# A gated delta layer: the decay table by a broadcast transfer and biased exponentials instead of matmuls

## The chip, the cores and the metric

The program runs on one core of one Trainium2 chip. The metric is the device time of one execution in microseconds (us). The kernel before has three runs; the median is what the kernel after is held against.

## What is computed

Two layers over `x` of 2 batches x 512 tokens x 256 features. Nearly all the time goes to the first: a gated delta rule with 16 key heads of 128, two value heads for each, and chunks of 64 tokens. For each head (T is a chunk's tokens):

```python
g = jnp.cumsum(g, axis=-1)                       # per chunk
diff = g[..., :, None] - g[..., None, :]
decay = jnp.where(tri, jnp.exp(jnp.where(tri, diff, 0.0)), 0.0)
M = jnp.where(tri_s, jnp.einsum('bhnci,bhndi->bhncd', k_b, k) * decay, 0.0)
Tinv = solve_triangular(eye + M, eye, lower=True)
u, w = Tinv @ v_b, Tinv @ (k_b * jnp.exp(g)[..., None])
attn_loc = jnp.where(tri, jnp.einsum('bhnci,bhndi->bhncd', q, k) * decay, 0.0)
# scan over chunks: v_new = u - w @ S; o = qg @ S + attn_loc @ v_new; S = S * exp(g_last) + kdecay^T @ v_new
og = o * silu(z); og = og * rsqrt(mean(og * og) + EPS) * norm_w;  y = og @ W_out
```

`q`, `k`, `v` go through a convolution of 4 taps and a silu first. Beside it stands a feed-forward layer with ternary weights (`f0`); then comes a second layer (attention, experts, a second ternary feed-forward), which the change leaves as it is.

## The kernel before

**Tiling.** The kernel works in blocks of 128 tokens, so a head has 2 batches x 4 blocks (`NT` = 8), and with its two value heads 16 tables of 128 x 128 (`HC` = 16). Everything is fp32. `gdn` holds the first layer. Each engine has its own streams of work, one generator per kind and head (`pe_decays`, `pe_key`, `pe_query`, `pe_value`, `pe_inverse`, `pe_z`, `pe_recur`, `pe_finish` on TensorE, and their fellows on the others).

**What sets the order.** Each piece of a stream yields a due time from a table written by hand (`AT` for heads 1 to 14, `FIRST` for head 0, `FINAL` for head 15, `START` for what runs once); head k adds `TURN * k`. `in_order` (L75) then puts the pieces of one engine in the order of their due times. So the tables set each engine's program order, and no more: on the chip an engine goes through its own list and waits on semaphores. The work of several heads is interleaved: while head k+1 makes its keys, queries and values, head k is inverted and runs its recurrence.

**One head.** `g_d` in device memory holds the cumulated gates of all heads as three bf16 parts.

- Decay table `E` (L545 to L557, L792 to L796): SyncE loads the head's rows of `g_d` into `GL` and `GR` (L478, L479). TensorE makes the differences in banks 2 and 3, four tables at a time: one matmul of 512 columns with the mask `later` (-1e30 above the diagonal), then four of 128 columns with the parts of g. ScalarE takes the exponential of 512 columns at once (L796). `E` is one buffer, so this waits for the last use of head k-1 (`AT`, L1000).
- Keys: projection (L542), first tap on ScalarE (L783), three taps on VectorE (L943), silu (L788), transposes into banks 2 and 3 (L571), squares and copies `kt` by ScalarE (L808, L815), scores k.k (L580). VectorE forms the norms (L948 to L973), GpSimd multiplies `E` by -beta/norm (`nE`, L1125), VectorE multiplies the scores by it: `CM` (L981).
- Queries likewise: scores q.k (L580) times `E` are `A` (L1000). Values: projections (L542), taps, transposes (L591), `vn` (L847).
- Inverse of I+M: `CM` goes to device memory and back as blocks of 16 (L507, L516), VectorE solves them (L1025 to L1031), they come back by DMA as `Td` (L525), and TensorE doubles the block size in `pe_inverse` (P16, TU16, P32, TU32, P64, U64: L597, L640, L647, L650, L653) with copies by ScalarE and VectorE between, all in banks 2 and 3. The scratch of it is `Td`, `Ud`, `P2`, `Tf`, `P4`, and the result is `UB`.
- Recurrence (L703 to L739): 8 steps (4 blocks x 2 batches); gate `z` (L690, L886); output: `og` is multiplied, normalised, transposed (L753), copied as `oT` (L935), projected (L761) and added to `yacc` (L1116).

GpSimd also does the ternary rounding of the f0 weights during head 0 and 1 (L1223 to L1231), and the f0 matmuls (L1367) fill TensorE during the recurrence of head 15.

## Time and profile before

| what | us |
|---|---|
| median of 3 runs | 1554.03 |
| lowest, highest run | 1548.35, 1557.99 |
| span of the profiled execution | 1551.7 |
| TensorE busy in it | 1401.1 (90%) |
| VectorE busy | 1046.9 (67%) |
| ScalarE busy | 865.6 (56%) |
| GpSimd busy | 534.3 (34%) |

The profiled execution's own time is its span from first to last instruction, 1551.7 us, with nothing else listed around it; it lies 2.3 us under the median. Busy shares are averages over stages that differ: until 120 us the heads start, until some 1100 us one head follows another in a steady pattern, until 1250 us the last head runs beside f0, and after it comes the second layer. A matmul's record includes its way through the array, so the time that a row of equal matmuls costs is read from start to start, not from the mean of one. One fp32 matmul of the program is two in the trace.

### The profile page before, as it was taken

Reading aid. Unit: us, or ns where it says so; the run is one execution under the profiler, and the core shown is the slowest. Engines: PE = TensorE matmul, PEld = TensorE weight load, DVE = VectorE, ACT = ScalarE, POOL = GpSimd, SP = SyncE. Lnnn points to the kernel's source line nnn. Section 1 sums busy time; section 2 is a strip of 40 time slices with the busy share of each in tenths; the row PEclk is TensorE's granted clock in tenths of the full one; section 3 lists DMA queues with packets and bytes.
Section 4 is the critical chain, followed back from the end, with each engine's and each line's share of the span. In section 5 each row is a group of like instructions: output and inputs, shape, how many; then the busy total and the mean of one; then the engine's idle time right before and its main releaser. Section 6 shows DMA issues by size and latency. Waiting matters only on the chain. (4 is left out here: it accounts for less than half of the span.)

```text
span 1551.7 us, 35674 instructions
## 1 busy us (share of the span) xinstructions
PE 1401.1 (90%) x13996; PEld 1045.2 (67%) x13996; DVE 1046.9 (67%) x2132; ACT 865.6 (56%) x1740; POOL 534.3 (34%) x562
## 2 busy tenths in 40 slices
PE   4569999999999999999999999999899977998998
PEld 3335767777776777777677777777578754555855
DVE  4887686877868687786858778686735544773344
ACT  5555656666666665666666666666355316676210
POOL 1872332342323233233323323333335446541100
PEclk9678999999999999999999999999989988999999
DMA  5112020201202021020102102110311130002100
GB/s 168 37 49 59 9 39 16 67 22 20 41 14 38 16 67 29 13 46 21 27 16 66 29 13 45 23 25 21 91 36 44 41 89 1 1 1 52 31 14 14
DMA packets 142486, 56.39 MB, mean 36 GB/s; under 512 B 109776, under 2 KB 134992, under 8 KB 142064
## 3 DMA queue, kind: packets, MB, share of 16 engines
q1 hardware_dynamic: 133424, 48.20, 13.4%
q10 hardware_dynamic: 8896, 5.91, 1.2%
q8 instruction: 113, 1.85, 0.5%
q14 instruction: 53, 0.43, 0.1%
HBM read 37.11 MB, written 16.97 MB: 35 GB/s over the span
## 5 line engine op out<-in xcount | busy, mean ns | idle before, releaser
L1153 POOL TENSOR_TENSOR og<-og,sz 128x256 f32<-128x256 f32 x128 | 93.3, 729 | 518.8 <-DVE og L1096 300.9
L690 PE MATMUL banks<-wz,xT 128*128 128x256 f32 x512 | 129.2, 397 | 13.8 <-DVE yacc L1116 13.8
L943 DVE SCALAR_TENSOR_TENSOR Yv<-banks,cwall,Yv 128x511 f32<-128x511 f32 (+2 forms) x192 | 130.3, 740 | 7.5 <-ACT Yv L783 7.4
L542 PE MATMUL banks<-wv,xT 128*128 128x512 f32 x256 | 121.5, 619 | 11.1 <-DVE Yv L943 9.6
L761 PE MATMUL banks<-wo,oT 128*128 128x256 f32 x512 | 123.8, 385 | 0.0
L542 PE MATMUL banks<-wqk,xT 128*128 128x512 f32 x256 | 121.7, 610 | 0.2 <-DVE Yk L943 0.2
L690 PEld LDWEIGHTS banks<-wz,xT 128*128 128x128 f32 x512 | 96.3, 196 | 36.6 <-issue 23.9
L930 ACT ACTIVATE junk<-og 128x512 f32<-128x512 f32 x64 | 40.6, 634 | 121.1 <-POOL og L1153 121.1
L1160 POOL TENSOR_TENSOR rn<-ss,c_half 128x4 f32<-128x4 f32 x64 | 64.5, 1007 | 122.0 <-DVE ss L1110 122.0
L761 PEld LDWEIGHTS banks<-wo,oT 128*128 128x128 f32 x512 | 93.6, 192 | 11.9 <-issue 0.7
L734 PE MATMUL banks<-V,A 128*128 128x128 f32 x512 | 85.8, 290 | 9.1 <-ACT V L910 9.1
L542 PEld LDWEIGHTS banks<-wv,xT 128*128 128x128 f32 x256 | 48.1, 198 | 61.6 <-issue 61.5
L1882 DVE TENSOR_REDUCE mx<-banks 128x1 f32<-128x128 f32 (+3 forms) x128 | 57.4, 487 | 43.5 <-PE banks L1805 43.1
L1082 DVE TENSOR_TENSOR St<-Sd,banks 128x256 f32<-128x256 f32 x64 | 26.9, 420 | 84.6 <-PE banks L739 84.6
L1125 POOL TENSOR_TENSOR E<-E,nsk 128x1024 f32<-128x1024 f32 x32 | 60.0, 1897 | 68.8 <-DVE nsk L970 51.3
L1107 DVE TENSOR_REDUCE ss<-junk 128x4 f32<-128x512 f32 x64 | 43.8, 684 | 56.9 <-ACT junk L930 56.9
L734 PEld LDWEIGHTS banks<-V,A 128*128 128x128 f32 x512 | 69.3, 191 | 18.5 <-ACT V L910 14.0
L542 PEld LDWEIGHTS banks<-wqk,xT 128*128 128x128 f32 x256 | 48.5, 196 | 43.4 <-issue 41.9
L935 ACT ACTIVATE oT<-banks,nw 128x512 f32<-128x512 f32 x64 | 44.4, 694 | 58.9 <-PE banks L753 58.9
L910 ACT COPY V<-banks 128x256 f32<-128x256 f32 x128 | 47.8, 374 | 48.2 <-PE banks L721 48.1
L943 DVE SCALAR_TENSOR_TENSOR Yk<-banks,cwall,Yk 128x511 f32<-128x511 f32 (+2 forms) x96 | 64.5, 740 | 6.1 <-ACT Yk L783 6.1
L721 PEld LDWEIGHTS banks<-R,UB 128*128 128x128 f32 x384 | 55.5, 193 | 19.3 <-issue 12.0
(380 smaller groups left out, 3663.2 us busy)
## 6 DMA issues: line engine op xcount, KB each, us to landing
cm_d<-CM SPq DMA_DIRECT2D x32, 256.0 KB, 4.0
wqk<-in_L_attn_W_qkvz SPq DMA_DIRECT2D x8, 512.0 KB, 4.6
wv<-in_L_attn_W_qkvz SPq DMA_DIRECT2D x8, 512.0 KB, 4.2
wz<-in_L_attn_W_qkvz SPq DMA_DIRECT2D x16, 256.0 KB, 2.9
wo<-in_L_attn_W_out SPq DMA_DIRECT2D x16, 256.0 KB, 3.1
blk<-cm_d SPq DMA_DIRECT2D x128, 16.0 KB, 1.8
t_d<-tb SPq DMA_DIRECT2D x16, 128.0 KB, 1.7
Td<-t_d SPq DMA_DIRECT2D x128, 16.0 KB, 1.9
```

Of the source, the lines that this page charges most:

```text
L542: ins = pe.matmul(bank[b][:, :], xT[:, d, b * S + of_batch, :], w[:, d, :], start=(d == 0), stop=(d == KD - 1))
L690: ins = pe.matmul(bank[7][:, b * 256:(b + 1) * 256], xT[:, d, b * S + q, :], wz[:, d, :], start=(d == 0), stop=(d == KD - 1))
L721: ins = pe.matmul(pV[:, h * DH:(h + 1) * DH], UB[k % 2][:, h * NT + n, :], R[b][:, h, :] if q else vn[k % 2][:, n, h, :], start=True, stop ...
L734: ins = pe.matmul(pK[:, h * DH:(h + 1) * DH], A[k % 2][:, h, n, :], V0[b][:, h, :], start=True, stop=True)
L761: ins = pe.matmul(bank[7][:, b * D:(b + 1) * D], oT[:, b, h, :], wo[k % 2][:, h, :], start=(h == 0), stop=(h == VR - 1))
L910: act.copy(V0[b][:, :, :], bank[6][:, 0:256].rearrange("p (h d) -> p h d", h=VR)).then_inc(s["V0"].sem, 1)
L935: act.activation(oT[:, :, :, :], bank[7][:, :].rearrange("p (b h t) -> p b h t", b=B, h=VR), ACT.Copy, scale=m["nw"][:, 0:1]).then_inc(s[" ...
L943: v.scalar_tensor_tensor(y, bank[b][:, 0:T - j], conv_w(k, t)[:, 3 - j:4 - j], y, ALU.mult, ALU.add).then_inc(s["tap"].sem, 1)
L1125: pool.tensor_tensor(E[:, h, :, :], E[:, h, :, :], nsk[:, h, :].unsqueeze(2).to_broadcast([P, NT, P]), ALU.mult).then_inc(s["nE"].sem, 1)
L1153: pool.tensor_tensor(og[:, n, :, :], og[:, n, :, :], sz[q % 2][:, b, :].rearrange("p (h d) -> p h d", h=VR), ALU.mult).then_inc(s["osz"].s ...
L1160: pool.tensor_tensor(rn[:, q, :, :], ss[:, q, :, :], c["neghalf"][:, 0:B * VR].rearrange("p (b h) -> p b h", b=B), ALU.pow).then_inc(s["rn ...
L1882: v.tensor_reduce(x[:, t, g:g + 1], top[i % 2][:, 0:(t + 1) * P], AX, ALU.max).then_inc(s["mx"].sem, 1)
```

## The change

1. The table `E` is made without TensorE. `g_d` keeps g as one fp32 row per head; SyncE loads it with one transfer that repeats the row to all 128 partitions, straight into `E` (1 MB a head). GpSimd adds the mask `later` (2 additions of 128 x 1024 a head, `pool_decays`), and ScalarE takes 16 exponentials of 128 x 128 in place, each with its own column of -g (`ngc`) as bias. `GL`, `GR`, their fills, the split into three bf16 parts and the 5 x 4 matmuls a head are gone.
2. The room goes to a second `CM`, and `Yq` gets a third buffer; `Tf` and `P4` become one tile `TP`.
3. With two `CM`, head k+1's k.k scores and `CM` come ahead of the inverse of head k: `P16` of head k now waits for `CM(1, k+1)`, and the k transposes of head k+1 no more for the end of head k's inverse but for `AT(1, k)`.
4. All due times of the first layer are new.

```diff
-    m["g_d"] = nc.dram_tensor("g_d", [3, HK, HC * P], BF16, kind="Internal").ap()
+    m["g_d"] = dram("g_d", [HK, HC * P])
+    m["ngc"] = sb("ngc", [P, W])
...
-        parts = Chain(v, s["pgp"])
+        v.tensor_scalar(m["ngc"][:, :], gc[:, :], -1.0, None, ALU.mult)
         yield START["gp"]
         v.wait_ge(*s["pgT"]())
-        v.tensor_copy(gT[:, :], bank[3][:, 0:W])
-        for i in range(3):
-            parts.step(v.tensor_copy(gp[:, i, :], bank[3][:, 0:W] if i == 0 else gT[:, :]))
-            if i < 2:
-                parts.step(v.tensor_tensor(gT[:, :], gT[:, :], gp[:, i, :], ALU.subtract))
+        v.tensor_copy(gT[:, :], bank[3][:, 0:W]).then_inc(s["pgp"].sem, 1)
...
-    "g": 115, "wqk": 137.01, "wv": 72.92, "cm": 160.76, "base": 209.71, "wz": 212.85, "E0": -33.56, "E1": -232.02, "E2": -29.83, "E3": -159.44, "exp0": -30.71, "exp1": -68.85,
+    "g": 14.39, "wqk": -22.77, "wv": 13.04, "cm": 30.79, "base": 76.04, "wz": 145.51, "E0": 10.19, "E1": 10.19, "exp0": 14.97, "exp1": 18.53, "exp2": 18.53, "exp3": 19.85,
...
         if k:
-            sp.wait_ge(*s["Ep"](3, k - 1))
+            sp.wait_ge(*s["AT"](1, k - 1))
         else:
-            sp.wait_ge(*s["zero"](1))
             sp.wait_ge(*s["pg_d"]())
-        sp.dma_start(GL[0:3, :, :], m["g_d"][:, k, :].rearrange("r (m t) -> r m t", t=P)).then_inc(s["gl"].sem, 16)
-        sp.dma_start(GR[3:6, :, :], m["g_d"][:, k, :].rearrange("r (m t) -> r m t", t=P)).then_inc(s["gl"].sem, 16)
+        sp.dma_start(Ef.rearrange("p m t -> p (m t)"), m["g_d"][k, :].partition_broadcast(P)).then_inc(s["gl"].sem, 16)
...
-    def pe_decay(pe, k, r):
...
-        pe.matmul(out[:, :], c["identb"][:, :], c["later"][:, :].unsqueeze(1).to_broadcast([P, 4, P]), start=True, stop=False, skip_group_check=True)
-        for j in range(4):
-            ins = pe.matmul(out[:, j * P:(j + 1) * P], GL[0:6, 4 * r + j, :], GR[0:6, 4 * r + j, :], start=False, stop=True, skip_group_check=True)
-        ins.then_inc(s["Ep"].sem, 1)
...
             if t == 0:
-                pe.wait_ge(*s["Eexp"](2 + half, k))
-                if k:
-                    pe.wait_ge(*s["U64"](1 - half, k - 1))
+                if k == 0:
+                    pe.wait_ge(*(s["pgp"]() if half else s["pact"](3)))
+                elif k == 1:
+                    pe.wait_ge(*s["U64"](1 - half, 0))
+                else:
+                    pe.wait_ge(*s["AT"](1, k - 1))
+            elif k < 2:
+                pe.wait_ge(*s["CM"](1, k))
             else:
-                pe.wait_ge(*s["CM"](1, k))
+                pe.wait_ge(*s["U64"](1 - half, k - 1))
...
-        pe.wait_ge(*(s["Eexp"](3, k + 1) if k + 1 < HK else s["AT"](1, k)))
+        pe.wait_ge(*(s["CM"](1, k + 1) if 0 < k < LAST else s["AT"](1, k)))
...
-            act.wait_ge(*s["Ep"](r, k))
-            if k and r == 0:
-                act.wait_ge(*s["AT"](1, k - 1))
-            act.activation(Ef[:, 4 * r:4 * r + 4, :], bank[2 + r % 2][:, :].rearrange("p (m i) -> p m i", i=P), ACT.Exp).then_inc(s["Eexp"].sem, 1)
+            act.wait_ge(*s["gm"](r // 2, k))
+            for i in range(4 * r, 4 * r + 4):
+                ins = act.activation(Ef[:, i, :], Ef[:, i, :], ACT.Exp, bias=m["ngc"][:, k * HC + i:k * HC + i + 1])
+            ins.then_inc(s["Eexp"].sem, 1)
...
-            if k and h == 0:
-                v.wait_ge(*s["P64p"](1, k - 1))
-                v.wait_ge(*s["cm_out"](1, k - 1))
-            v.tensor_tensor(CM[:, h, :, :], pair3, E[:, h, :, :], ALU.mult).then_inc(s["CM"].sem, 1)
+            if k >= 2 and h == 0:
+                v.wait_ge(*s["P64p"](1, k - 2))
+                v.wait_ge(*s["cm_out"](1, k - 2))
+            v.tensor_tensor(CM[k % 2][:, h, :, :], pair3, E[:, h, :, :], ALU.mult).then_inc(s["CM"].sem, 1)
...
+    def pool_decays(pool, k):
+        for h in range(VR):
+            yield at(k)[f"E{h}"]
+            pool.wait_ge(*s["gl"](0, k))
+            part = E[:, h, :, :]
+            pool.tensor_tensor(part, part, c["later"][:, :].unsqueeze(1).to_broadcast([P, NT, P]), ALU.add).then_inc(s["gm"].sem, 1)
```

**TensorE, before**, where head k+1's decay matmuls stand in a middle head (L761 is the output projection, L734, L739 and L703 the recurrence):

```order
L761 MATMUL banks<-wo,oT 128x256 [waits oT]
L761 MATMUL banks<-wo,oT 128x256 x3
L555 MATMUL banks<-c_later,c_identb 128x512 [waits AT,gl]
L557 MATMUL banks<-GR,GL 128x128 x4
L555 MATMUL banks<-c_later,c_identb 128x512
L557 MATMUL banks<-GR,GL 128x128 x4
L734 MATMUL banks<-V,A 128x128 [waits og,AT,V0]
L734 MATMUL banks<-V,A 128x128
L739 MATMUL banks<-V,kt 128x256 [waits V2]
L703 MATMUL banks<-St,Yk 128x256 [waits og,S]
L703 MATMUL banks<-St,Yq 128x256
L555 MATMUL banks<-c_later,c_identb 128x512 [waits Eexp]
```

**TensorE, after**, from the second half of head k+1's query projection (L540) over its k.k scores (L568) to the next output projection (L744):

```order
L540 MATMUL banks<-wqk,xT 128x512 [waits tap]
L540 MATMUL banks<-wqk,xT 128x512
L568 MATMUL banks<-Yk 128x128 [waits kt]
L568 MATMUL banks<-Yk 128x128 x3
L568 MATMUL banks<-Yk 128x128 [waits kt]
L568 MATMUL banks<-Yk 128x128 x3
L736 MATMUL banks<-c_ident,og 128x128 [waits z,wo,ogn]
L736 MATMUL banks<-c_ident,og 128x128 x3
L704 MATMUL banks<-R,UB 128x128 [waits V2,S,V0,R]
L704 MATMUL banks<-R,UB 128x128
L744 MATMUL banks<-wo,oT 128x256 [waits oT]
L744 MATMUL banks<-wo,oT 128x256 x3
```

No decay matmul is left. The k.k scores stand here ahead of `P16` of head k, which comes 11 rows further down; before, they stood behind the last matmul of that inverse.

**ScalarE, before**, at the exponentials (L796) of a middle head, and what is next on it (L902 is `QS`, L910 the copy `V0`, L935 the copy `oT`):

```order
L796 ACT_TABLE_LOAD [waits AT]
L796 ACTIVATE E<-banks 128x512 [waits Ep] x4
L930 ACTIVATE junk<-og 128x512 [waits red,osz]
L902 ACTIVATE QS<-banks,tab 128x128 [waits og,R]
L902 ACTIVATE QS<-banks,tab 128x128
L910 COPY V<-banks 128x256 [waits AV,TR]
```

**ScalarE, after**, at the same work (L778), from the last three of the first four exponentials to the copy `oT` (L918):

```order
L778 ACTIVATE E<-E,ngc 128x128 x3
L791 ACTIVATE sq<-banks 128x512 [waits nqs,kTp]
L798 COPY kt<-banks 128x512 [waits SU]
L791 ACTIVATE sq<-banks 128x512 [waits kTp]
L798 COPY kt<-banks 128x512
L766 ACTIVATE Yq<-banks,cwall 128x512 [waits proj,KSp]
L766 ACTIVATE Yq<-banks,cwall 128x512 [waits proj]
L778 ACTIVATE E<-E,ngc 128x128 [waits gm]
L778 ACTIVATE E<-E,ngc 128x128 x3
L778 ACTIVATE E<-E,ngc 128x128 [waits gm]
L778 ACTIVATE E<-E,ngc 128x128 x3
L918 ACTIVATE oT<-banks,nw 128x512 [waits wout,oTp]
```

The first four exponentials now stand ahead of the squares and copies of k, and eight more ahead of `oT`.

**GpSimd, after**, in a middle head (before, it had only the L1125 pair here; L1143 and L1139 are the gate product and the state's decay, L1150 and L1154 the output's normalisation):

```order
L1143 TENSOR_TENSOR og<-og,sz 128x256 [waits z,og]
L1139 TENSOR_TENSOR Sd<-St,tab 128x256 [waits S]
L1108 TENSOR_TENSOR E<-E,c_later 128x1024 [waits gl] x2
L1150 TENSOR_TENSOR rn<-ss,c_half 128x4 [waits ms]
L1154 TENSOR_TENSOR og<-og,rn 128x2x256 [waits rn]
```

The two additions wait for the transfer, and the normalisation of the output is queued behind them.

## Rows read from the trace of the kernel before

**Rows 1.** Busy time in stretches: us, busy of each engine, TensorE clock, DMA share, GB/s.

```profile
core 0: us, PE busy (x) PEld busy (x) DVE busy (x) ACT busy (x) POOL busy (x), PEclk, DMA share, GB/s
...
50.00:120.00 70.00, 44.56 (x559) 30.11 (x559) 56.82 (x70) 36.41 (x55) 54.93 (x28) 0.70 0.18 45
120.00:980.00 860.00, 818.78 (x9281) 625.96 (x9282) 644.27 (x1305) 537.64 (x1131) 277.86 (x300) 0.99 0.16 32
980.00:1150.00 170.00, 156.15 (x1867) 121.11 (x1867) 114.13 (x227) 96.03 (x211) 54.65 (x56) 0.95 0.16 37
```

**Rows 2.** Who TensorE waited for from 120 to 980 us: total, times, longest.

```profile
PE banks L690 <- DVE yacc L1116: 8.5, 12, 1.6
PE banks L734 <- ACT V L910: 8.0, 24, 0.5
PE banks L597 <- issue: 6.6, 4, 1.9
PE banks L753 <- ACT sz L886: 5.3, 12, 0.4
PE banks L597 <- DMA Td<-t_d: 3.7, 6, 1.0
```

**Rows 3.** The instructions that write or read `CM`: number, duration, first to last start.

```profile
L981 DVE TENSOR_TENSOR CM<-banks,E x32: 1212/1218/1225, 64.9 to 1082.4; 128x1024 f32<-128x1024 f32 x32
```

**Rows 4.** TensorE in order of time, decay matmuls: start, us, what, idle before.

```profile
628.47 0.38 PE L555 MATMUL banks<-c_later,c_identb 128*128 128x512 bf16 x1
...
629.42 0.39 PE L557 MATMUL banks<-GR,GL 6*128 6x128 bf16 x4
629.75 0.71 PE L734 MATMUL banks<-V,A 128*128 128x128 f32 x4
```

**Rows 5.** TensorE in order of time, a projection and what follows.

```profile
612.76 3.60 PE L542 MATMUL banks<-wv,xT 128*128 128x512 f32 x8
616.19 1.89 PE L690 MATMUL banks<-wz,xT 128*128 128x256 f32 x8
```

**Rows 6.** Groups by line: busy us, mean ns of one, idle before.

```profile
L1125 POOL TENSOR_TENSOR E<-E,nsk 128x1024 f32<-128x1024 f32 x32 | 60.0, 1897 | 68.8 <-DVE nsk L970 51.3 <-issue 17.1 <-POOL Yk L1231 0.4
...
L920 ACT ACTIVATE V<-banks,skd 128x128 f32<-128x128 f32 x192 | 61.3, 379 | 0.0
...
L796 ACT ACTIVATE E<-banks 128x512 f32<-128x512 f32 x64 | 37.6, 597 | 28.4 <-PE banks L557 27.5
...
L796 ACT ACT_TABLE_LOAD x16 | 20.5, 1283 | 5.4 <-DVE A L1000 5.1
```

**Rows 7.** DMA issues: number, KB each, median us to landing.

```profile
A<-in_L_ffn_w_gate_up SPq DMA_DIRECT2D x1, 1024.0 KB, 5.9
...
og<-in_L_ffn_w_proj SPq DMA_DIRECT2D x1, 1024.0 KB, 14.1
...
UB<-in_L_ffn_w SPq DMA_DIRECT2D x1, 1024.0 KB, 5.5
```

**Rows 8.** VectorE in order of time, the `A` products and six taps of k.

```profile
621.94 2.36 DVE L1000 TENSOR_TENSOR A<-banks,E 128x1024 f32<-128x1024 f32 x2
...
666.71 4.02 DVE L943 SCALAR_TENSOR_TENSOR Yk<-banks,cwall,Yk 128x511 f32<-128x511 f32 x6
```

**Rows 9.** GpSimd in order of time, the same form twice.

```profile
45.84 1.89 POOL L1225 TENSOR_TENSOR A<-A,qscale 128x1024 bf16<-128x1024 bf16 x1
...
54.44 2.76 POOL L1225 TENSOR_TENSOR A<-A,qscale 128x1024 bf16<-128x1024 bf16 x1
```

**Rows 10.** Who TensorE waited for from 0 to 200 us.

```profile
PE banks L555 <- DMA GR<-g_d: 9.2, 2, 8.5
PE banks L542 <- DVE Yv L943: 8.3, 1, 8.3
PE banks L571 <- ACT Yq L788: 8.2, 1, 8.2
...
PE banks L555 <- ACT E L796: 2.8, 2, 2.3
```

More of the change, by code:

```diff
@@ L511, in sp_blocks @@
         else:
[L512 removed]
+            sp.wait_ge(*s["zero"](0))
         for q in range(8):
@@ L598, in pe_blocks @@
         return ins
-    def pe_decays(pe, k):
-        for r in range(4):
-            yield at(k)[f"E{r}"]
-            pe_decay(pe, k, r)
     def pe_key(pe, k):
@@ L639, in pe_inverse @@
             for lo, hi in (quarters[0:2], quarters[2:4]):
-                ins = pe.matmul(b3[hi, i * C:(i + 1) * C], CMf[lo, i, hi], Td[lo, i, :], start=True, stop=True)
+                ins = pe.matmul(b3[hi, i * C:(i + 1) * C], cm[lo, i, hi], Td[lo, i, :], start=True, stop=True)
         ins.then_inc(s["P32p"].sem, 1)
@@ L681, in pe_z @@
                 pe.wait_ge(*s["y"](q - 2, k))
-            elif k:
-                pe.wait_ge(*s["y"](2 + q, k - 1))
+            elif k > 1 or k and not q:
+                pe.wait_ge(*s["y"](2 + q if k > 1 else 3, k - 1))
             elif q:
@@ L873, in act_inverse @@
             act.wait_ge(*s["P64p"](r, k))
-            act.copy(P4[halves[1], 8 * r:8 * r + 8, :], wide(out)[halves[1], :, :]).then_inc(s["P64"].sem, 1)
+            act.copy(TP[halves[1], 8 * r:8 * r + 8, :], wide(out)[halves[1], :, :]).then_inc(s["P64"].sem, 1)
         for r, out in enumerate((bank[3], bank[2])):
```

94 lines of the change are left out of this document (43 added, 51 removed), and 80 rows, old and new, of tables (AT, ATTN, FINAL, FIRST).

## Prediction

> **What bounds the kernel now.** I read the busy time in stretches first. From 120 to 980 us, where one head follows another, TensorE is busy 818.8 of 860 us at a granted clock of 0.99, VectorE 644.3, ScalarE 537.6 and GpSimd 277.9 [rows 1]: TensorE bounds this stage, and its idle time is 41.2 us. The products `CM` give the length of a head: from the first to the last start lie 1017.5 us, less one product of 1.2 us, over 15 heads, so 67.8 us a head [rows 3]. The idle time is thus 41.2 / (860 / 67.8) = 3.2 us a head. Who TensorE waited for says how it is made up: the five largest waits make 32.1 of the 41.2 us, none longer than 1.9 us [rows 2]. So a gain must come from work taken off TensorE, and any new wait on it is paid in full. At the start it is otherwise: from 50 to 120 us TensorE is busy 44.6 of 70 us at a clock of 0.70, VectorE 56.8, GpSimd 54.9 [rows 1].
>
> **The decay matmuls go.** Two of a head's four groups stand from 628.47 to the next matmul's start at 629.75, 1.28 us [rows 4]; four groups are 2.56 us, and 16 heads 41.0 us. That is the whole gross gain. (The busy columns would say more, since the records overlap.)
>
> **What the table costs instead.** ScalarE: 16 exponentials of 128 x 128 with a column as bias. The trace has none from SBUF with a bias; the nearest row is the copy of 128 x 128 with a column as scale, 61.3 us for 192, so 0.32 us each in a row and 0.38 alone [rows 6]. I take 0.32, so 5.1 us a head, against 37.6 / 16 = 2.35 us now [rows 6]: 2.8 us more, at most 3.7 with 0.38. ScalarE has room on the whole (63% busy [rows 1]); what counts is who stands behind. GpSimd: two additions of 128 x 1024, like the product `nE` at 1.90 us [rows 6], 3.8 us a head on an engine with 32% load [rows 1]. The transfer: 1 MB in `E`. Transfers of 1 MB took 5.5 and 5.9 us in quiet and 14.1 among others at the start [rows 7]; none of these repeats a row. I take 5.9, since the new one stands alone in its place, and keep 5.5 and 14.1 as ends. The DVE steps of the split at the start, and the fills, are worth some 2 us once.
>
> **A head walked through in the new order.** A projection's 8 matmuls of 512 columns go from 612.76 to 616.19 [rows 5]: 0.43 us for 512 columns, 0.215 for 256, 0.11 for 128. Let t = 0 be the start of the second half of head k's q.k scores.
>
> - The scores take 0.9 us, the two `A` products 2.36 [rows 8], so `E` is free at 3.3. The transfer lands at 9.2, the additions end at 11.1 and 13.0.
> - TensorE's list from there to head k+1's k transposes: scores 0.9, half of the k projections' program rows twice (3.4), output projection 1.7, gate 1.7, three rounds of the recurrence 6.1, transposes 0.5, together 14.3. VectorE's six taps of k (4.0 us [rows 8]) and the silus end at 14.8, just in time. ScalarE then loads the exponentials' table, 1.28 us [rows 6], and is ready at 16.1. The additions are there since 11.1: 5.0 us to spare, so up to a transfer of 10.9 us no one waits for it.
> - Four exponentials (1.3), the four squares and copies of k (1.9, each of 512 columns like the 0.6 of the exponential of today [rows 6], overlapping), two first taps of q (1.3), eight exponentials (2.6): 23.2. Then comes `oT` at 23.8. TensorE has done q's projection and the k.k scores at 20.6 and wants `oT` at 21.5: a new wait of 2.3 us.
> - The last exponentials end at 25.1, the second `nE` product at 27.0, `CM` at 28.2 [rows 3, 6]. TensorE gets to `P16`, where it now waits for that `CM`, at 31.5: hidden by 3.3 us. Queued behind `P16` are the recurrence and the value projection, so they would be late next.
> - VectorE goes from `CM` through an addition to `yacc`, the state and six taps of v to `T16` at 36; TensorE is at `P32` at 35.3: 0.7. Later the solve of the blocks and two transposes (`U32`) stand on VectorE ahead of `PU64`: 1.1.
>
> New waits 4.1 us a head. Of today's 3.2 us the places are all rearranged, so I set the one against the other: 0.9 us more. A head is 2.56 - 0.9 = 1.66 us shorter; 14 heads (2 to 15) give 23.2 us.
>
> **SyncE's queue.** The transfer waits for `A`, and behind it stand `CM`'s way to memory, which needs the table anyway, and the loads of `wz`, `wo`. `Td` of head k is now due about 50 us after its `CM`, so the way through memory has slack.
>
> **Start and end.** In the first 200 us TensorE waits 9.2 us for the rows of g and 2.8 for exponentials [rows 10]; both waits lose their object, with 5.1 us of matmuls. But VectorE and GpSimd are full there [rows 1], the two heads put 7.6 us of additions between GpSimd's ternary steps, and the waits for taps and silus (8.3 and 8.2 us [rows 10]) only end earlier if VectorE does. Bounds: -17 to +8; I take -4. At the end the last head's inverse moves to a later place, beside fewer matmuls: -1, bounds -6 to +6.
>
> One thing speaks against the additions. The same GpSimd form took 1.89 us at 45.84 and 2.76 us at 54.44 [rows 9], while VectorE was busy on the k chain. The Trainium skill (GPSIMD Engine Reference, Specifications) says that GpSimd's SBUF interfaces are shared with VectorE, with contention when VectorE runs instructions with two SBUF inputs. By the row without contention head 0's additions cost 3.8 us, by the contended one 5.5. In later heads VectorE's work at that time (taps, `yacc`) reads one input from PSUM, so by the rule too they should keep 1.90; the sum changes by under 2 us.
>
> **Sum.** 1551.7 - 23.2 - 4 - 1 = 1523.5 us for a profiled execution; the median of the runs lies 2.3 above this execution's span, so 1526.
>
> **Rivals.**
> A. *All of it hides.* The wait for `oT` needs ScalarE late by more than TensorE's other small waits; if it and the two on VectorE fall into pauses that are there anyway, a head gains the full 2.56 (35.8 in 14), and the start gives the 12 us of waits in rows 10: 1554 - 48 = 1506. For it: the new order no longer ties k's scores to the inverse. Against: ScalarE's extra 2.8 us stands on the k chain itself.
> B. *Handed back.* TensorE gains 2.56 but waits as much more behind the exponentials, if each takes 0.38 rather than 0.32 (0.9 us), and VectorE's clump from `nk` to `T16` (17 us of its work against 15 of TensorE's) costs 0.8 more: 0.0 a head, start -4: 1550.
> C. *Slower: the transfer is late.* One mechanism: 128 partitions read the same 8 KB, and if that is as slow as the 14.1 us row, the additions end at 19.3 instead of before 16.1; ScalarE stands in front of the k copies, so scores, `CM` and `P16` shift 3.2 us a head. Less 1.66 that is +1.5 x 14 = +21, start -4: 1571. It decides from 12.6 us on (10.9 that hide, 1.7 that the matmuls pay).
> That the change doesn't do what it says is no rival: the listed order has no decay matmul left.
>
> **From cases to numbers.** Forecast 0.50 (own range 1512 to 1539), A 0.15, B 0.20, C 0.15. The range leaves out half of C and the far end of A: 1496 to 1567. About 1% (15.5 us) is what a measurement can tell from no change. Faster by more: A and nearly all of the forecast, 0.62; within: B and little of the others, 0.22; slower: C and a rest, 0.16.
>
> **What would show it.** Right: the head 66.1 us long; matmuls L744 waiting some 2 us a head for `oT`; the transfer landing in about 6 us; GpSimd's additions at 1.90; `P16` not waiting for `CM`. Wrong: scores L568 waiting for `kt` and ScalarE for the additions (C); many more waits for VectorE's `T16` and `U32` (B); TensorE idle under 2.5 us a head (A); the first `CM` after 70 us, or a clock under 0.70 for longer than from 50 to 120 us.

## The result, and the profile after

| | median us | lowest, highest | runs |
|---|---|---|---|
| before | 1551.19 | 1547.58, 1557.99 | 4 |
| after | 1566.44 | 1562.32, 1571.19 | 4 |

The ratio is 1.0097 [1.0068, 1.0125]: slower by 1.0%, where 1526 us was forecast. The profiled execution has a span of 1560.6 us against 1551.7, so 8.9 us of the 15 can be looked for in the trace.

Busy time in the same stretches as [rows 1], kernel after:

```profile
50.00:120.00 70.00, 27.86 (x389) 18.07 (x389) 57.34 (x64) 24.48 (x45) 58.52 (x29) 0.67 0.22 59
120.00:980.00 860.00, 792.98 (x8954) 614.08 (x8951) 661.26 (x1292) 558.29 (x1282) 330.06 (x317) 0.96 0.20 46
```

Three things stand out. From 50 to 120 us TensorE did 389 records instead of 559. In the steady stretch it is idle 67.0 us instead of 41.2. And its clock there is 0.96 instead of 0.99.

Who TensorE waited for from 120 to 980 us, kernel after (total, times, longest), which answers to [rows 2]:

```profile
PE banks L744 <- ACT oT L918: 18.4, 12, 1.6
PE banks L585 <- issue: 16.4, 13, 2.2
PE banks L636 <- ACT TP L857: 8.6, 13, 0.7
PE banks L717 <- ACT V L893: 5.5, 4, 3.5
PE banks L623 <- issue: 5.5, 5, 2.0
PE banks L704 <- DVE R L1058: 5.4, 2, 4.6
PE banks L633 <- DVE UB L1040: 2.4, 4, 0.8
```

And the instructions on `CM`, which answer to [rows 3], kernel after:

```profile
L964 DVE TENSOR_TENSOR CM<-banks,E x32: 1210/1215/1225, 71.3 to 1085.5; 128x1024 f32<-128x1024 f32 x32
```

A head is (1085.5 - 71.3 - 1.2) / 15 = 67.5 us long instead of 67.8, where 66.1 was forecast. (Heads 2 to 15 alone: 67.2 and 67.35.) The first `CM` starts 6.4 us later, the last 3.1 us later, and the span ends 8.9 us later.

Where it went, with the forecast's own split:

- **Start.** The value projection of head 0 starts at 106.8 us instead of 95.7. The `CM` of head 2 starts at 210.4 instead of 205.6: +4.8, forecast -4.
- **Heads.** From there to the last `CM`, 13 heads: 874.0 instead of 875.6 us, so -1.6, forecast 13 x -1.66 = -21.6.
- **After the last `CM`**: +5.7, forecast -1, and the 14th head's -1.66. No run looks into this part by itself.

The marks are not quite the same place in the two kernels: in the new order `CM` of a head stands ahead of the inverse of the head before it. So some of what lies behind the first mark in the kernel after lay ahead of it in the kernel before. The start lost more than the 4.8 us (the value projection says 11.1), and the part after the last `CM` less than 5.7.

The heads hold two things that the forecast did not have. The first is the line "issue" above: pauses of TensorE within a run of 32 x 32 matmuls, with nobody to wait for. They were 6.6 us at 4 places [rows 2] and are 16.4 + 5.5 = 21.9 us at 18. The second is the clock. I summed (1 - granted clock) times length over stretches of 3 us from 200 to 1100 us, and call it the clock loss: 3.4 us before, 25.6 after, in seven stretches at the half clock (1.2 GHz). It is an upper bound of what the clock costs, since it also counts time in which TensorE has nothing to do. One such place, TensorE in order of time in the kernel after (start, us, what, idle before):

```profile
413.62 1.29 PE L585 MATMUL banks<-Td,CM 32*32 32x32 f32 x128
414.87 0.68 PE L704 MATMUL banks<-R,UB 128*128 128x128 f32 x4
415.59 0.89 PE L585 MATMUL banks<-P,Ud 32*32 32x32 f32 x81
417.98 0.61 PE L585 MATMUL banks<-P,Ud 32*32 32x32 f32 x47 [1.50 <-issue]
...
423.95 4.97 PE L540 MATMUL banks<-wv,xT 128*128 128x512 f32 x8
```

and the same microseconds in the windows view, after:

```profile
419.00:421.00 2.00, 2.00 (x63) 1.64 (x64) 1.90 (x5) 1.32 (x3) 0.00 (x0) 0.72 0.30 32
421.00:423.00 2.00, 2.00 (x18) 1.85 (x14) 1.78 (x8) 1.96 (x4) 0.00 (x0) 0.50 0.81 256
```

The first 128 narrow matmuls are P16 (`Td`, `CM`), the other 128 are TU16 (`P`, `Ud`); 0.7 us of wider ones stand between them. TensorE pauses 1.5 us in TU16, and 2 us after the pause it runs at the half clock; the projection's 8 matmuls behind it take 4.97 us instead of the 3.60 of [rows 5]. All seven half-clock stretches begin beside such a pause, of 1.15 to 2.17 us. But TU16 also pauses in five heads (0.98 to 1.51 us) in which the clock stays up, so a pause of this length goes with the drop and does not settle it.

### The profile page after: what moved, and what is told of

The parts are those of the page before. It is cut to its first block and busy times, and to the rows that moved or that the text cites. A ratio compares the mean times of both kernels' runs of the same rounds, so it can differ in the third digit from the quotient of the medians.

```text
span 1560.6 us, 35246 instructions
## 1 busy us (share of the span) xinstructions
PE 1366.2 (88%) x13676; PEld 1032.1 (66%) x13676; DVE 1073.1 (69%) x2128; ACT 893.3 (57%) x1932; POOL 603.3 (39%) x592
## 3 DMA queue, kind: packets, MB, share of 16 engines
q1 hardware_dynamic: 134960, 64.52, 16.4%
## 5 line engine op out<-in xcount | busy, mean ns | idle before, releaser
L1143 POOL TENSOR_TENSOR og<-og,sz 128x256 f32<-128x256 f32 x128 | 93.1, 727 | 509.0 <-DVE og L1079 389.9
L744 PE MATMUL banks<-wo,oT 128*128 128x256 f32 x512 | 124.6, 385 | 20.4 <-ACT oT L918 20.4
L540 PE MATMUL banks<-wv,xT 128*128 128x512 f32 x256 | 124.9, 633 | 17.1 <-DVE Yv L926 15.7
L673 PE MATMUL banks<-wz,xT 128*128 128x256 f32 x512 | 139.0, 398 | 0.0
L540 PE MATMUL banks<-wqk,xT 128*128 128x512 f32 x256 | 121.4, 607 | 9.9 <-DVE Yk L926 9.9
L744 PEld LDWEIGHTS banks<-wo,oT 128*128 128x128 f32 x512 | 93.2, 190 | 40.4 <-ACT oT L918 23.1
L673 PEld LDWEIGHTS banks<-wz,xT 128*128 128x128 f32 x512 | 93.5, 197 | 17.1 <-issue 6.7
L540 PEld LDWEIGHTS banks<-wv,xT 128*128 128x128 f32 x256 | 52.5, 208 | 70.7 <-issue 68.8
L1150 POOL TENSOR_TENSOR rn<-ss,c_half 128x4 f32<-128x4 f32 x64 | 64.6, 1009 | 81.5 <-DVE ss L1093 80.2
L1099 DVE TENSOR_TENSOR yacc<-yacc,banks 128x512 f32<-128x512 f32 x64 | 43.8, 684 | 73.1 <-PE banks L744 72.7
L717 PEld LDWEIGHTS banks<-V,A 128*128 128x128 f32 x512 | 74.4, 196 | 20.4 <-ACT V L893 15.8
L778 ACT ACTIVATE E<-E,ngc 128x128 f32<-128x128 f32 x256 | 79.8, 405 | 0.2
L540 PEld LDWEIGHTS banks<-wqk,xT 128*128 128x128 f32 x256 | 46.2, 195 | 49.8 <-issue 49.4
L1108 POOL TENSOR_TENSOR E<-E,c_later 128x1024 f32<-128x1024 f32 x32 | 75.1, 2365 | 2.6 <-DMA E<-g_d 2.3
L885 ACT ACTIVATE QS<-banks,tab 128x128 f32<-128x128 f32 x192 | 59.3, 363 | 17.1 <-DVE R L1058 17.1
```

What stands on the lines that cost most here:

```text
L540: ins = pe.matmul(bank[b][:, :], xT[:, d, b * S + of_batch, :], w[:, d, :], start=(d == 0), stop=(d == KD - 1))
L673: ins = pe.matmul(bank[7][:, b * 256:(b + 1) * 256], xT[:, d, b * S + q, :], wz[:, d, :], start=(d == 0), stop=(d == KD - 1))
L717: ins = pe.matmul(pK[:, h * DH:(h + 1) * DH], A[k % 2][:, h, n, :], V0[b][:, h, :], start=True, stop=True)
L744: ins = pe.matmul(bank[7][:, b * D:(b + 1) * D], oT[:, b, h, :], wo[k % 2][:, h, :], start=(h == 0), stop=(h == VR - 1))
L778: ins = act.activation(Ef[:, i, :], Ef[:, i, :], ACT.Exp, bias=m["ngc"][:, k * HC + i:k * HC + i + 1])
L885: ins = act.activation(QS[b][:, h, :], bank[4 + b][:, 256 + h * DH:256 + (h + 1) * DH], ACT.Copy, scale=tab[:, k, EG, h, n:n + 1])
```

## The experiments

Each is against runs of the kernel before on the same chip, whose medians were 1553.1 (e), 1552.3 (f), 1554.2 (g) and 1551.5 us (h). The clock losses are each from one profiled execution. The record also has the mean granted clock of every execution, over the whole program; its medians are used beside them. Of edits to due times only the changed entries are printed, with their table in brackets.

### e1: the wait for oT

ScalarE copies `oT` ahead of the third and fourth group of exponentials.

```diff
-"exp2": 18.53   (AT)
+"exp2": 19.8
```

> The changed kernel, but in heads 1 to 14 ScalarE copies oT ahead of the third and fourth group of exponentials of the next head, not between them. Theory: in the changed kernel TensorE waits 1.5 us for this copy in every head (18.4 us from 200 to 980 us); the last exponential ends when it did, so nothing else comes later. Then that wait falls below 0.5 us a head and the kernel gains 1.1 x 14 = 15 us. Rival: TensorE is held by what comes behind (the scratch TP, the copies V, the pauses inside the 32 x 32 matmuls), which take up the gain: 0 to 3 us faster.

Measured: 1570.74 us, 1.0142 [1.0075, 1.021], no gain. TensorE's waits from 120 to 980 us in e1:

```profile
PE banks L585 <- issue: 19.8, 13, 2.2
PE banks L717 <- ACT V L893: 19.1, 16, 3.5
...
PE banks L744 <- ACT oT L918: 4.8, 12, 0.4
```

`oT` falls from 18.4 to 4.8 us, and 13.6 us appear at `V` instead (5.5 to 19.1): in this order the exponentials stand before one of the two. The theory (15 us faster) fell, its rival (0 to 3 us faster) too by its number.

### e2: the pauses

P16 moves into the middle of the value projection, so that half of the projection stands between P16 and TU16.

```diff
-"pv2": 25.11, "pv3": 25.11   "P16": 97.28, "P16x": 97.28   (AT)
+"pv2": 25.2,  "pv3": 25.2    "P16": 95.0,  "P16x": 95.0
```

> The changed kernel, but in heads 1 to 14 P16 (128 records of 32 x 32) stands in the middle of the value projection, so that 1.8 us of 512-column matmuls come between it and TU16 (128 more). In the changed kernel TensorE pauses 0.7 to 2.2 us inside these matmuls, in 16 places from 200 to 980 us, 19.7 us, with no releaser; before it did so in 4 places, 6.6 us. Theory S (spacing): 256 tiny matmuls in a row are used up faster than instructions arrive; the pauses fall under 8 us and the half-clock stretches that follow them become fewer: 10 to 20 us faster. Theory D (transfers): the pauses come because the store of CM and the loads of the blocks run at the same moment; the pauses stay above 15 us, within 3 us of the changed kernel.

Measured: 1568.9 us, 1.0076 [1.0044, 1.0109]. The waits in e2:

```profile
PE banks L623 <- DVE Td L1020: 14.0, 11, 2.3
PE banks L704 <- DVE R L1058: 10.7, 8, 3.6
...
PE banks L585 <- issue: 5.5, 4, 2.6
...
PE banks L623 <- issue: 2.4, 2, 2.1
```

The pauses fall from 21.9 to 5.5 + 2.4 = 7.9 us at 6 places, so the spacing of the narrow matmuls bears on them. The gain goes to the next in line: VectorE's `T16` copy (L1020) and `R` are late now. The clock loss stays at 25.6 us, the same as in after: waits for VectorE have taken the place of the pauses, and the clock drops all the same. So the pauses are not what the clock alone hangs on. The theory (10 to 20 us faster, fewer half-clock stretches) fell.

### e3: transfers as the cause of the pauses

`CM`'s way to memory waits until the inverse before it has passed its TU16.

```diff
 def sp_blocks
+        if k > 1:
+            sp.wait_ge(*s["T16p"](0, k - 1))
```

> The changed kernel, but SyncE stores CM of head k (k of 2 and more) only after TU16 of head k-1, so that neither the store nor the loads of the blocks run beside the 256 tiny matmuls. Theory D (transfers): the pauses without a releaser fall from 19.7 us to under 6 us and the granted clock from 200 to 980 us rises from 0.97 to 0.99 or more: 15 to 25 us faster, if the blocks' later arrival (about 8 us) stays hidden. Theory S (spacing): the pauses stay above 15 us; time the same, or up to 10 us slower by the solve of the blocks.

Measured: 1677.94 us, 1.0805 [1.077, 1.0841]; waits in e3:

```profile
PE banks L706 <- DVE R L1060: 57.4, 10, 7.9
...
PE banks L587 <- issue: 15.8, 11, 2.1
...
PE banks L625 <- issue: 5.3, 6, 1.1
```

The pauses stay (21.1 us) though the transfer is gone from beside them: around the one that ends at 448.5 us the DMA share is 0.00 from 447.0 to 448.6. So transfers are not their cause. The delayed store itself costs 1677.9 - 1566.4 = 112 us against after. It goes out 8.6 us after its `CM` instead of at once, and a head is (1197.0 - 71.4 - 1.2) / 15 = 75.0 us long, 7.5 us more. VectorE waits 84.6 us for the blocks, with the `R` that TensorE needs queued behind. The 50 us of slack that the prediction gave `Td` are not slack of VectorE's queue, which has next to none. Clock loss 76.8 us, with waits of up to 7.9 us.

### e4: the order of the start

```diff
-"exp0".."exp3": 34.38, "nk": 45     (FIRST)
+"exp0".."exp3": 29.6,  "nk": 40.5
-            yield START["qt"] + GROUPS[g]
+            yield START["qt"] + GROUPS[g] + (2.4 if g == 1 else 0.0)
```

> The changed kernel with three places of head 0 in another order: the k.k scores ahead of the second transpose of the ternary weights on TensorE, the exponentials ahead of the silu of q on ScalarE, the norms of k ahead of the taps of q on VectorE. Theory: the first CM starts 5 us earlier (66 for 71.3 us), everything behind it too, and the kernel is 4 to 6 us faster. Rival: the start is bound by VectorE and GpSimd in front of each other's transfers and not by CM; CM moves, the second pair of taps of the values (now 103.3 us) does not: 0 to 1 us.

Measured: 1573.23 us, 1.0137 [1.0089, 1.0185]. The first `CM` moves from 71.3 to 70.4 us and the second tap of v from 103.3 to 102.7: the order of the exponentials is at most a small part of what made the start late.

### f1 and f2: the new table in the old order

f1 is the kernel before with only the table changed (transfer, additions, 16 exponentials). Its order is else as before, but for the exponentials, which stand one right behind the other. f2 makes each head's transfer in two halves, the first as soon as the first `A` product has read its half of `E`. Cut from f1's edit, then from f2's against f1:

```diff
-            sp.wait_ge(*s["Ep"](3, k - 1))
+            sp.wait_ge(*s["AT"](1, k - 1))
...
-    def pe_decays(pe, k):
...
-            sp.wait_ge(*s["AT"](1, k - 1))
+            sp.wait_ge(*s["AT"](0, k - 1))
```

> The kernel before, with only its decay table made anew (broadcast transfer, two additions on GpSimd, 16 biased exponentials): one CM, all else in the old order, the exponentials where they stood, for head 1 behind the last part of the inverse. No decay matmul is left. Theory: the new order and not the new table costs the time. TensorE loses 2.56 us of matmuls a head; the exponentials (5.0 us for 2.4, and not before 631.5 on the old time axis) hold ScalarE's copies of V back by some 1.3 us, so a head is 1.0 to 1.5 us shorter: 12 to 20 us faster than before. Rival: the table is what costs; the period stays at 67.6 us a head (0 to 5 us faster), because TensorE waits out what it no longer computes, at a lower clock.

> As f1_table_only, but the transfer in two halves of 512 KB, the first as soon as the first A product has read its half of E. Theory: the additions start 2 to 3 us earlier and ScalarE's exponentials no more hold V back: 3 to 10 us faster than f1_table_only. Rival: ScalarE's own 5.0 us is what holds, not the arrival: within 3 us of f1_table_only.

Measured: f1 1618.8 us, 1.0423 [1.0375, 1.0471]; f2 1639.21 us, 1.0551 [1.05, 1.0602]. GpSimd and VectorE in order of time and TensorE's longest wait, in f1:

```profile
520.32 6.19 POOL L1103 TENSOR_TENSOR E<-E,c_later 128x1024 f32<-128x1024 f32 x2 [3.50 <-DMA E<-g_d]
```

```profile
521.90 2.38 DVE L1008 TENSOR_TENSOR t<-tb,p 128x512 f32<-128x512 f32 x1
```

```profile
PE banks L668 <- DVE yacc L1094: 54.0, 11, 7.8
```

and VectorE and the same wait in f2:

```profile
382.89 2.77 DVE L1009 TENSOR_TENSOR t<-blk,tb 128x512 f32<-128x512 f32 x1
```

```profile
PE banks L671 <- DVE yacc L1097: 72.4, 11, 7.8
```

`A` of the head before is done at 515.3 us, the transfer lands at 520.3, and the additions end at 526.5. In the old order the new table is 66 us slower, so the reordering is no extra of this change, it is what carries it. But the longest wait is not one for the table. h3 below has no late table and shows the same wait for `yacc` at 37.3 us. The rest of it comes from VectorE: the additions on GpSimd now run beside its solve of the blocks, in every head. In f1 a product that takes 1.08 us in the kernel before takes 2.38. In f2 the additions come earlier (380.0 to 384.8 us at this head) and hit a second product too, 2.77 us instead of 1.03. The solve grows by 1.6 us a head in f1 and 3.4 in f2 (means of 12 heads), and a head of f1 and f2 is 2.5 and 3.8 us longer than one of h3 (71.8, 73.2 and 69.3 us by the `CM` starts). The theory of f2 fell: an earlier table made the kernel slower, because of what its additions run beside.

### f3: the start, calm

In both kernels GpSimd's ternary steps run beside VectorE's solve of the blocks of head 0. VectorE in order of time, kernel after:

```profile
85.81 2.07 DVE L1008 TENSOR_TENSOR t<-blk,tb 128x2 f32<-128x2 f32 x1
87.91 0.16 DVE L1009 TENSOR_REDUCE tb<-t 128x2 f32<-128x2 f32 x1
88.10 1.98 DVE L1008 TENSOR_TENSOR t<-blk,tb 128x8 f32<-128x8 f32 x1
```

and GpSimd at the same time:

```profile
85.34 2.51 POOL L1219 TENSOR_TENSOR vn<-vn,UB 128x1024 bf16<-128x1024 bf16 x1
87.93 2.12 POOL L1221 TENSOR_TENSOR UB<-UB,vn 128x1024 bf16<-128x1024 bf16 x1
```

VectorE's two products end at 87.88 and 90.08, each within 0.04 us of the end of GpSimd's instruction (87.85, 90.05): they wait until it is through. Six of the seven small products of the solve take 1.8 to 2.1 us.

f3 holds GpSimd's last group of ternary steps back until that solve is done.

```diff
             yield then + 4.0
+            if g == 3:
+                pool.wait_ge(*s["sub"](17, 0))
```

> The changed kernel, but GpSimd makes the last two steps of the fourth group of ternary weights, and all behind them, only after VectorE has solved head 0's blocks of 16. Theory: six of VectorE's small steps there take 1.8 to 2.1 us each and not the 0.2 us that they take in later heads, because GpSimd's products of 128 x 1024 run beside them; alone the solve takes 9 us for 17.4 us, the taps of the values and all behind come 7 us earlier, and the kernel is 5 to 8 us faster. Rival: the small steps are slow for another reason: the solve stays at 15 us or more, and the kernel is up to 8 us slower by GpSimd's wait.

Measured: 1562.85 us, 1.0062 [1.0037, 1.0087]. VectorE in f3:

```profile
85.88 0.15 DVE L1008 TENSOR_TENSOR t<-blk,tb 128x2 f32<-128x2 f32 x1
...
92.89 4.03 DVE L926 SCALAR_TENSOR_TENSOR Yv<-banks,cwall,Yv 128x511 f32<-128x511 f32 x6
```

The solve takes 7.0 instead of 17.4 us (12.7 in the kernel before), and head 2's `CM` starts at 199.0 instead of 210.4. The Trainium skill (GPSIMD Engine Reference, Specifications) has the rule that the two engines share their SBUF interfaces and that VectorE's instructions with two SBUF inputs contend: the trace agrees, since the reductions between, with one input, take 0.16 us either way. Of the 11 us won at the start the ratio keeps some 5 (1.0062 against 1.0097), and as the two intervals overlap, a gain in the time of the whole is not shown by this run alone. The profiled execution, one of its slower ones, gives them back later, with a clock loss of 41.0 us.

### f4: matmuls in the wait for oT

The transposes of `og` are done four times over instead of once, which puts 1.3 us of matmuls a head (18 us in all) in front of the wait for `oT`. The extra ones write the same values again.

```diff
-            for b in range(B):
+            for b in [b for _ in range(4 if q == 1 and 0 < k < LAST else 1) for b in range(B)]:
```

> The changed kernel, but in heads 1 to 14 TensorE makes the second group of transposes of og four times over, 1.3 us of matmuls more a head just ahead of its 1.55 us wait for oT. Theory: the wait takes these matmuls in for nothing (wait 0.3 us), the half-clock stretches become fewer (25.6 us lost by them from 200 to 1100 us in the changed kernel, 3.4 us before), and the time is the same or up to 12 us less although 18 us of work came in. Rival: the clock does not hang on this pause: the loss stays at 20 us or more, time within 3 us of the changed kernel; or the work is paid in full, 18 us slower.

Measured: 1563.05 us, 1.0064 [1.0036, 1.0091], with a wait for `oT` of 4.9 instead of 18.4 us. 18 us of matmuls cost nothing: the `oT` wait is idle time that nothing on TensorE is late for. The clock loss of 11.9 us is that of its fastest execution (1549.11 us, mean clock 0.952). The median of its ten executions is 0.942, hardly above after's 0.94, so that the filler helps the clock is not shown.

### g1 to g4, h1 and h2: together and apart

"Calm" is f3's edit, "filler" f4's. "Pause" moves TU16 and P32 one step back, so that more wide matmuls stand between the narrow runs, without moving P16 as e2 does:

```diff
-"TU16": 97.82, "TU16x": 97.82   "P32": 99.78    (AT)
+"TU16": 98.9,  "TU16x": 98.9    "P32": 101.0
```

g1: calm, filler and pause. g2: the kernel before, with calm alone. g3: pause alone. g4: calm and pause, with the third exponentials at 19.8 and the fourth at 22.0. h1: calm and pause. h2: g1 with e4's start.

> The changed kernel with GpSimd's wait of f3_calm, the filler of f4_filler and the order of g3_pause together. Theory: the start gives 11 us back, the pauses 10 us, and with TensorE denser the half-clock stretches cost under 12 us from 200 to 1100 us: 20 to 25 us faster than the changed kernel, so 5 to 10 us faster than the kernel before. Rival: the granted clock takes back what the start gives (40.9 us lost by it in f3_calm): within 5 us of the changed kernel.

> The kernel before, with GpSimd's wait of f3_calm (the last two steps of the fourth group of ternary weights, and what is behind, only after head 0's blocks are solved). Theory: the clash of VectorE's small steps with GpSimd stands in the kernel before as well, where the solve takes 12.7 us; alone it takes 7.0 us: 3 to 6 us faster than before. Rival: the start of the kernel before is bound elsewhere, or GpSimd's later ternary work is missed: 0 to 3 us slower.

> The changed kernel, but in heads 1 to 14 the second half of the z projection stands ahead of TU16 and not behind it, and a product of V and two of the state stand ahead of P32. Theory: with 2.8 us of wide matmuls between P16 and TU16 the pauses without a releaser fall from 19.7 us to under 10, and no new wait takes their place as it did in e2_spread (the copy of T16 has 1.4 us more): 5 to 12 us faster than the changed kernel. Rival: the next wait takes it, or the clock: within 3 us.

> The changed kernel with GpSimd's wait of f3_calm and the order of g3_pause, and ScalarE's four groups of exponentials in heads 1 to 14 spread: the third behind the copy of oT, the fourth behind the copies of V. Theory: the wait for oT falls from 1.5 to 0.4 us a head and, other than in e1_ot_ahead, no wait for V takes its place; 25 us faster than the changed kernel, 10 us faster than the kernel before. Rival: CM, which now comes 1.2 us later, holds P16, or the clock takes the gain: within 5 us of g1_three or slower.

> g1_three without the filler (GpSimd's wait of f3_calm and the order of g3_pause). Theory: the filler pays by the clock alone. Without it the half-clock stretches from 200 to 1100 us cost 10 to 20 us more than the 8.5 us of g1_three, and the kernel is 5 to 12 us slower than g1_three, though TensorE has 18 us less to do. Rival: the filler does nothing once the pauses are short: within 2 us of g1_three.

> g1_three with the three reorderings of e4_start in head 0. Theory: with GpSimd out of the way, head 0's chain through CM decides, CM comes 1 us earlier and the kernel is 1 to 3 us faster than g1_three. Rival: TensorE's waits for GpSimd's ternary weights decide: the same within 1 us.

Between kernels of different groups the ratios are what compares:

| | median us | ratio to before | clock loss us, one execution | mean clock, median of all executions |
|---|---|---|---|---|
| before | 1551.5 to 1554.2 | 1 | 3.4 | 0.960 |
| after | 1566.44 | 1.0097 [1.0068, 1.0125] | 25.6 | 0.940 |
| f3 calm | 1562.85 | 1.0062 [1.0037, 1.0087] | 41.0 | 0.943 |
| f4 filler | 1563.05 | 1.0064 [1.0036, 1.0091] | 11.9 | 0.942 |
| g3 pause | 1553.44 | 0.9991 [0.9968, 1.0014] | 5.1 | 0.954 |
| g4 calm, pause, late exponentials | 1563.79 | 1.0075 [1.0048, 1.0102] | 20.5 | 0.948 |
| h1 calm, pause | 1540.91 | 0.9929 [0.9909, 0.9948] | 5.1 | 0.958 |
| g1 calm, pause, filler | 1536.61 | 0.9892 [0.9867, 0.9918] | 8.5 | 0.958 |
| h2 the same, start of e4 | 1531.32 | 0.987 [0.9834, 0.9906] | 3.4 | 0.963 |
| g2 before, calm | 1551.37 | 0.9986 [0.9969, 1.0003] | 3.1 | 0.960 |

The last column does not rest on one execution: the clock of after is lower than that of before in every execution on record (0.938 to 0.945 against 0.956 to 0.964), and the pause order brings most of it back.

TensorE in order of time in g3, the same place as shown of after:

```profile
414.78 1.29 PE L585 MATMUL banks<-Td,CM 32*32 32x32 f32 x128
416.03 0.68 PE L704 MATMUL banks<-R,UB 128*128 128x128 f32 x4
416.55 1.03 PE L673 MATMUL banks<-wz,xT 128*128 128x256 f32 x4
417.51 0.85 PE L585 MATMUL banks<-P,Ud 32*32 32x32 f32 x77
418.76 0.64 PE L585 MATMUL banks<-P,Ud 32*32 32x32 f32 x51 [0.40 <-issue]
```

and the windows and waits of g3:

```profile
120.00:980.00 860.00, 792.86 (x9030) 614.31 (x9026) 667.91 (x1305) 564.56 (x1301) 334.67 (x323) 0.98 0.20 47
```

```profile
PE banks L585 <- issue: 11.6, 13, 1.7
...
PE banks L633 <- DVE UB L1040: 7.5, 10, 0.8
...
PE banks L623 <- issue: 5.5, 6, 1.9
```

Here the pause is 0.40 instead of 1.50 us and no half clock follows. This is the best of its places: over 11 heads the pauses in TU16 are 0.9 us in the mean instead of 1.4. Over the stretch g3's pauses fall only from 21.9 to 17.1 us and `UB` takes that back: TensorE is idle for 67 us as in after. What differs is the clock, 0.98 instead of 0.96, and with it 76 more records done in the same 860 us. g3 is 1% faster than after by the ratios (13 us by the medians). Its profiled span is 16.7 us shorter, and its clock loss 20.5 us smaller; both are the fastest executions of their kernels.

Calm gives 0.6% more on top (h1, the intervals apart), which it did not clearly do alone. The filler's 4.3 us (g1 against h1 by the medians) are not seen in the spans (1535.9 and 1535.8 us), so that term stays unclear. g4 shows the rival of e1 again: with the exponentials put back, `oT` waits only 4.7 us but `R` 12.5, the clock loss is 20.5, and 23 of h1's us are gone. It shows more: P16 and TU16 stand apart in g4 as in h1, and still its pauses are 22.4 us (h1: 15.1), one of 2.29 us within the first 128 narrow matmuls. So spacing is not all that they depend on. The kernel before gains nothing clear of noise from calm (g2), though its solve takes 8.9 us instead of 12.7.

h2 has the lowest median: 1531.32 us (1528.67 to 1538.14), 1.3% under before and 2.2% under after; its interval overlaps g1's. `CM` in h2:

```profile
L964 DVE TENSOR_TENSOR CM<-banks,E x32: 1205/1216/1225, 70.6 to 1058.9; 128x1024 f32<-128x1024 f32 x32
```

Its head is (1058.9 - 70.6 - 1.2) / 15 = 65.8 us, at a clock of 0.99 from 120 to 980 us.

### h3: the gross gain alone

The kernel before without the decay matmuls of heads 1 to 15. It leaves the decay out there (the exponentials run with scale 0), so its time is that of the old order with 15 x 2.56 = 38 us of matmuls and the small transfers of g taken away, and nothing put in.

```diff
-        for r in range(4):
+        for r in range(0 if k else 4):
```

> The kernel before without the decay matmuls and the transfers of g's rows of heads 1 to 15: ScalarE takes its exponentials of 128 x 512 of what stands in the banks, with scale 0 (it leaves the decay out of these heads). Nothing else is moved. Theory: this is the gross gain by itself. If TensorE bounds the steady stage and no wait grows, a head loses 2.56 us and the kernel is 33 to 38 us faster than before. Rival: the other waits and the granted clock take part of it back already here, with no new table, no new order and no second CM: under 20 us faster.

Measured: 1576.57 us, 1.0146 [1.0104, 1.0188]: slower, with 38 us less to do. TensorE's longest wait in h3:

```profile
PE banks L692 <- DVE yacc L1119: 37.3, 11, 4.2
```

VectorE and then TensorE in order of time, h3:

```profile
639.59 0.16 DVE L1028 TENSOR_TENSOR t<-blk,tb 128x2 f32<-128x2 f32 x1 [1.22 <-DMA blk<-cm_d]
...
646.62 0.69 DVE L1119 TENSOR_TENSOR yacc<-yacc,banks 128x512 f32<-128x512 f32 x1
```

```profile
647.46 3.42 PE L692 MATMUL banks<-wz,xT 128*128 128x256 f32 x8 [3.67 <-DVE yacc L1119]
```

and TensorE at this place in the kernel before:

```profile
632.55 0.39 PE L557 MATMUL banks<-GR,GL 6*128 6x128 bf16 x4
633.94 1.97 PE L690 MATMUL banks<-wz,xT 128*128 128x256 f32 x8 [1.00 <-DVE yacc L1116]
```

The gate's matmuls need the bank that VectorE empties into `yacc`, and that addition stands behind the solve (639.6 to 646.6), which waits for its DMA. In the kernel before all four groups of a head's decay matmuls stood ahead of this wait, beside the solve (628.47 and 631.59 on; the solve from 626.1 to 633.1), and filled that hole: the wait was 1.00 us there, and is 3.67 here. Over the stretch it was 8.5 us [rows 2] and is 37.3: 28.8 us more, 2.6 for each of its 11 places, as much as the decay matmuls of a head [rows 4]. On top comes the clock: the 8 matmuls behind the wait run at the half clock (3.42 us instead of 1.97), the clock loss is 23.8 us against 3.4, and a head is (1105.9 - 64.8 - 1.2) / 15 = 69.3 us long instead of 67.8. In the old order the matmuls were free.

## Why the prediction was wrong, by its steps

By the spans 37 us are missing between the forecast 1523.5 and the 1560.6 measured: 20 in the heads, 8.8 at the start and 8.4 after the last `CM`, by the marks above.

**"A gain must come from work taken off TensorE, and any new wait on it is paid in full", with 41.0 us as "the whole gross gain".** This is the step that failed first. TensorE busy 95% of a stretch does not make each matmul a cost. In the order of before, h3 takes 38 us away and gets slower. In the new order f4 puts 18 us in and costs nothing. The small waits in [rows 2], which I read as proof of a saturated engine, were small because matmuls filled the holes. In the new order the work did go, TensorE's busy time a head falling from 64.6 to 62.0 us (818.8 and 793.0 of 860 us, by heads of 67.8 and 67.2), but 2.0 of these 2.6 us came back as idle time, 3.2 to 5.2 us a head.

**"Of today's 3.2 us the places are all rearranged, so I set the one against the other: 0.9 us more."** This is the term of the sum that was mis-sized: 2.0 us more in after. The new waits that it lists came to less than its 4.1 us, 1.8 in all (below). What it had at nothing came instead: the pauses in the narrow matmuls, 1.7 us a head where the kernel before had 0.5, and a wait of 0.7 us for ScalarE's copy `TP`.

**The clock was a term at nothing as well.** I took 0.99 as given while I changed the order that gives it. Over the 13 heads the clock loss grew by 22.2 us, which is an upper bound; the 1.1 us a head of idle time above the forecast are 14 us more, and the two together are more than the 20 us missing, so they can't be added. That the clock is a real part of it, g3 shows by one edit: as much idle time, a higher clock, 13 us faster.

**"A head is 1.66 us shorter."** Its head of 66.1 us is reached once the order is mended, but not in after. g3's head is (1072.3 - 71.2 - 1.2) / 15 = 66.7 us, and 66.2 over heads 2 to 15. The `CM` line of g3:

```profile
L964 DVE TENSOR_TENSOR CM<-banks,E x32: 1211/1218/1227, 71.2 to 1072.3; 128x1024 f32<-128x1024 f32 x32
```

In after the head is 67.2.

**The terms one by one.** The groups of the page that belong to them, kernel after:

```profile
L778 ACT ACTIVATE E<-E,ngc 128x128 f32<-128x128 f32 x256 | 79.8, 405 | 0.2
...
L1108 POOL TENSOR_TENSOR E<-E,c_later 128x1024 f32<-128x1024 f32 x32 | 75.1, 2365 | 2.6 <-DMA E<-g_d 2.3
...
E<-g_d SPq DMA_DIRECT2D x16, 1024.0 KB, 4.8
```

- Exponentials: 79.8 / 256 = 0.31 us each. Right (0.32).
- Additions: 2.35 us each. Wrong (1.90); the mask's broadcast operand or company may be why, which no run tells apart. 0.9 us a head of the 5.0 to spare, so it cost nothing in the steady stretch.
- Transfer: 4.8 us. I took 5.9. Rival C falls: the k scores never waited for it.
- `oT`: 18.4 / 12 = 1.5 us a head against 2.3. Right in place, and by f4 not a cost at all.
- `P16` never waited for `CM`. Right. `T16`: 1.0 us over the stretch, not 0.7 a head. `U32` (the wait for `UB`): 2.4 / 12.8 = 0.2 a head, not 1.1.
- Not in the sum: the wait for `TP` (8.6 us, 0.7 a head), the pauses (21.9 us against 6.6), the clock.

**"Start -4."** It was +4.8 at head 2's `CM`, 11.1 at the value projection. The prediction's own sign of a bad start came true: the first `CM` after 70 us (71.3), the clock from 50 to 120 us under 0.70 (0.67). The working counted the additions' 7.6 us between the ternary steps, and left it at that. But with the additions ahead of them other ternary steps stand beside VectorE's solve: six of its products take 2 us each, 17.4 - 7.0 = 10.4 us in all, where 12.7 - 7.0 = 5.7 were lost before. The solve also began 6.3 us later (85.8 against 79.5). TensorE waited there:

```profile
PE banks L540 <- DVE Yv L926: 15.7, 1, 15.7
```

which was 8.3 us before [rows 10]. [Rows 9] had shown the clash, but I priced it only on GpSimd's side, where it is the smaller, and I misread its company. At the slow 54.44 us VectorE was not on the k chain but on two ternary products with two inputs from SBUF (52.42 to 58.28, 5.86 us, where the same two took 2.36 at 41.42). The taps of k stood beside the fast one at 45.84. So VectorE's side of the clash was in the trace of before. f3 shows this step by a single edit as to the solve (7.0 us) and head 2's `CM` (11.4 us earlier); as to the time of the whole it is shown only on top of the pause order (h1 against g3, 0.6%). (Why the solve began later was not tried, but for e4's 0.9 us at the first `CM`, behind which it began no earlier.)

**The rivals.** B (1550, nothing gained in a head, start -4) had the heads nearly right, and for other reasons: neither the exponentials nor VectorE's clump took the gain. A is refuted by the median, yet h2's 1531.32 lies between A and the forecast, so the matmuls removed are worth something in the right order. That the calm, spaced kernels come near the forecast is no merit of the sum, which had no term for what they mend.

What stays open: why the narrow matmuls pause. Spacing bears on them (e2) but does not fix them (g4), transfers do not cause them (e3), and the profile shows no releaser. Nor is it settled which idle time drops the clock. In after the drops stand beside the pauses; in h3, e2 and e3 beside waits for VectorE. The pause order went with a loss of 3.4 to 8.5 us in four kernels and of 20.5 in g4, and the old order with 3.4 and 3.1, but 23.8 in h3 and 35.1 in f1, where TensorE waits for `yacc`.

## What to carry to other kernels

Before an engine's work is priced as gain, look at what the other engines do beside it: work that fills a wait is free, and to take it away only makes the wait visible; one run that leaves the work out tells the gross gain before any replacement is built. An order with as much idle time can have a lower clock, so read the granted clock of an order, not only its waits, and read it from several executions: one execution of f4 had a clock of 0.952 where the median is 0.942. Where GpSimd gets new work, look at which VectorE instructions with two inputs from SBUF it now runs beside: here that lengthened the start, and most of what a head of f1 and f2 is longer than one of h3.
